# Pacing token scatters and gathers beside attention by a raw-product signal in place of a score signal

## What is computed

```python
x = x + 0.5 * _L0_ffn_ref(_layernorm(x), gate_w, expert_bias, w1, w2)
x = x + _L0_attn_ref(_layernorm(x), Wq, bq, Wk, bk, Wv, bv, Wo, bo, prior_lambda)
x = x + 0.5 * _L0_ffn_ref(_layernorm(x), gate_w, expert_bias, w1, w2)
...
# attention: 16 heads of 8 channels
scores = jnp.einsum('bhqd,bhkd->bhqk', Q, K) / math.sqrt(hd)
scores = scores + prior_lambda * _gaussian_mask(Lx)[None, None, :, :]
attn = jax.nn.softmax(scores, axis=-1)
...
# experts: 8 real ones and 4 that pass x through, the best 2 per token
topk_logits, topk_idx = jax.lax.top_k(logits, TOP_K)
```

## Time and profile before

| | us |
|---|---|
| median of 3 runs | 1354.19 |
| lowest and highest run | 1350.55, 1358.74 |
| span of the profiled execution | 1338.4 |
| TensorE, VectorE, ScalarE, GpSimd busy in it | 1003.1, 906.0, 716.5, 621.8 |

### The profile page before, as it was taken

The page is one execution under the profiler, slowest core; times in us unless marked ns, Lnnn a source line. Parts: engine busy times, 40 slices in busy tenths (PEclk is TensorE's granted clock), DMA queues, the critical chain, the costliest instruction groups (busy, mean ns, idle before and its releaser), DMA issues.

```text
span 1338.4 us, 37494 instructions
## 1 busy us (share of the span) xinstructions
PE 1003.1 (75%) x13558; PEld 656.9 (49%) x13558; DVE 906.0 (68%) x2405; ACT 716.5 (54%) x1486; POOL 621.8 (46%) x697
## 2 busy tenths in 40 slices
PE   1468587788778888888888888898888876774770
PEld 1346243475447544574444754454754465433560
DVE  4548776685566787866887758877867853654524
ACT  1157344567355755667556575555675555442650
POOL 2556256404544544354542544544445445543554
PEclk9989699998788999998999889988999987785886
DMA  8354535352135311362112731123621274130464
GB/s 247 78 125 107 152 98 173 70 131 55 58 68 131 84 52 60 82 149 60 48 58 65 141 87 53 47 61 73 137 81 53 62 162 113 48 90 19 110 145 113
DMA packets 248881, 125.30 MB, mean 94 GB/s; under 512 B 124384, under 2 KB 238925, under 8 KB 248448
## 3 DMA queue, kind: packets, MB, share of 16 engines
q1 hardware_dynamic: 232320, 94.01, 27.2%
q0 software_dynamic: 16384, 28.89, 8.9%
HBM read 36.25 MB, written 65.31 MB: 76 GB/s over the span
## 4 chain that ended last, share of the span: by engine, by line
PE 39%; DVE 27%; issue 15%; ACT 8%; another core or an unknown queue 7%; POOL 2%; DMA 1%; SPq 1%; DVEq 0%; POOLq 0%; ACTq 0%
PE banks L594 10%; DVE row_max L1329 9%; PE banks L623 4%; PE banks L569 3%; ACT probs L849 3%; DVE h_lo L1223 3%; PE banks L561 2%; PE banks L474 2%; ACT h_hi L778 2%; PE banks L431 2%; PE banks L472 2%; PE banks L487 2%; PE banks L490 2%; DVE stats L1094 2%
## 5 line engine op out<-in xcount | busy, mean ns | idle before, releaser
L849 ACT ACTIVATE probs<-banks 128x512 f32<-128x512 f32 x512 | 280.1, 595 | 313.0 <-PE banks L594 270.4
L1329 DVE TENSOR_REDUCE row_max<-banks 128x2 f32<-128x512 f32 x512 | 330.9, 685 | 100.5 <-PE banks L594 65.2
L938 POOL DMA_INDIRECT big<-yg,slots x256 | 255.2, 997 | 278.3 <-ACT y_rows L784 84.0
L924 POOL DMA_INDIRECT xg<-xs,slots x256 | 253.6, 991 | 274.7 <-PE banks L594 167.8
L1223 DVE TENSOR_TENSOR h_lo<-h_f,h_hi 128x512 bf16<-128x512 f32 x198 | 134.5, 688 | 156.7 <-ACT h_hi L778 118.5
L623 PE MATMUL banks<-probs,v_op 128*32 128x256 f32 x2048 | 202.2, 413 | 10.7 <-ACT ot_sb L842 3.0
L569 PE MATMUL banks<-q_op,k_op 32*128 32x256 bf16 x1024 | 152.2, 293 | 64.7 <-issue 46.0
L594 PE MATMUL banks<-band_parts,thirds 96*32 96x296 bf16 (+2 forms) x4096 | 189.7, 294 | 1.3 <-issue 1.3
L487 PE MATMUL banks<-w_all,h_hi 128*128 x792 | 157.6, 229 | 43.1 <-DVE h_lo L1223 21.6
L561 PE MATMUL banks<-k_op,q_in 32*128 32x256 bf16 x1024 | 154.7, 295 | 37.8 <-DVE row_max L1329 31.5
L776 ACT ACTIVATE h_f<-banks 128x512 f32<-128x512 f32 x198 | 119.8, 605 | 114.3 <-PE banks L474 71.5
(11 more groups left out here) (173 smaller groups left out, 1668.6 us busy)
## 6 DMA issues: line engine op xcount, KB each, us to landing
yg<-y_rows SPq DMA_DIRECT2D x198, 128.0 KB
k_op<-kq_kept SPq DMA_DIRECT2D x96, 64.0 KB
q_in<-kq_kept SPq DMA_DIRECT2D x96, 64.0 KB
xg<-zeros SPq DMA_DIRECT2D x2, 2944.0 KB
xg<-xs,slots POOLq DMA_INDIRECT x256
big<-yg,slots POOLq DMA_INDIRECT x256
kq_kept<-kq_hi SPq DMA_DIRECT2D x32, 128.0 KB
kq_kept<-kq_lo SPq DMA_DIRECT2D x32, 128.0 KB
```

Source lines behind the costliest of these rows:

```text
L849: act.activation(probs[:, q % 2, u % 4, :], banks[:, ST[(16 * b + u) % 3], :], ACT.Exp).then_inc(A["exp_done"], 1)
L924: pool.indirect_dma_start(xg[q], bass.IndirectOffsetOnAxis(slots[:, q % 4, c, t:t + 1], 0), xs[:, q % 2, t, :], None, bounds_check=groups[ ...
L938: pool.indirect_dma_start(y_back[:, i, c, :], None, yg[q], bass.IndirectOffsetOnAxis(slots[:, q % 4, c, t:t + 1], 0)).then_inc(gathered[i] ...
L1329: dve.tensor_reduce(row_max[:, gp, :, qt, j], banks[:, MX[v % 2], :].rearrange("p (k c) -> p k c", k=2), AX.X, ALU.max).then_inc(A["max_do ...
```

## The change

Within `spread` alone, each transfer waits for another signal. So far, if both transfers of a tile fall into one step, the first waits for the step's first score signal and the second for its second; if they fall into two steps, each waits for the second score signal of its own step. Now, if both fall into one step, they wait for the step's first and second raw-product signal; if into two, each waits for the first raw-product signal of its own step. Where no raw products are left for the step (the steps from the eleventh on after the start of turn 30), both wait for the first score signal.

```diff
-                    same = at[0] == at[1]
-                    counts = [16 * b + 2 * at[0] + (1 if same else 2), 16 * b + 2 * at[1] + 2]
-                    rows(q, t, t + 1, (A["st_done"], *counts))
+                    if 16 * b + 2 * at[1] + 12 <= 16 * NBATCH:
+                        same = at[0] == at[1]
+                        counts = [16 * b + 2 * at[0] + 11, 16 * b + 2 * at[1] + (12 if same else 11)]
+                        rows(q, t, t + 1, (A["raw_done"], *counts))
+                    else:
+                        counts = [16 * b + 2 * at[0] + 1, 16 * b + 2 * at[1] + 1]
+                        rows(q, t, t + 1, (A["st_done"], *counts))
```

## The result

The changed kernel took 1375.89 us (median of 4 runs, 1372.63 to 1384.16) against 1354.61 us for the kernel before in the same set (4 runs, 1350.55 to 1358.74). The ratio is 1.0152, with a 95% interval of 1.0107 to 1.0198: about 21 us slower. The profiled execution has a span of 1372.8 us. Executions that the record marks as slow count in the medians but not in the ratios.

A forecast was written before the change was run, and what follows sets the result against it. TensorE and VectorE were taken to bound the kernel, with GpSimd early and waiting for TensorE. Terms 0 + 0 + 0 + 0 on a 1338.4 us span, 15.8 us below the median, gave 1354 us; range 1344 to 1363.

The forecast's parts named there:

- the slower side: Measured times above 1361 us, given a chance of 0.15: most of the slower rival and as much of the forecast's tail.
- the term of traffic: Transfers beside the next sequence's operand-row loads: one random 0.92 us hold of TensorE per turn, 0 us, 5 us either way.
- The start of the transfers: Paced transfers on GpSimd: some 167 of 288 start 0.3 to 0.8 us sooner; in turn 14, within 0.9 us of first maximum.
- Ends of gathers: Gathers beside attention end up to 0.8 us sooner, three steps or more ahead of use in combine: 0 us.
- the experts' columns: Column loads behind a segment's last scatter start 0.8 us sooner, 7 us ahead of the first expert matmul: 0 us.
- What is queued behind the waits: GpSimd's next transfer and norm: at most 12 norms start sooner, meeting VectorE's column operation or not; 5.4 us either way, taken 0.
- Slower rival, operand rows: Step 0's earlier transfer delays operand rows TensorE needs in step 3: 14 us added, 1368, or 1361 with half; chance 0.14.
- Faster rival: Transfers leave the crowded end of a step: norms gain up to 5.4 us, holds 9.2 us; near 1343; chance 0.20.
- the rule weighed with it: GpSimd and VectorE lock a shared port pair; transfers belong beside maxima, not combine. By the rule alone, time stays 1354.
- What would make it wrong: The prediction's last sentence: a hold of TensorE that no row names follows the timing of the transfers.
- the smaller signs: GpSimd's busy time falls by under 20 us, chain share near 2%; VectorE's and TensorE's busy times the same to 1%.

The follow-up runs named there:

- experiment A: The change applied to step 7's transfers alone, and to all but step 7's; against the kernel before in a 1350 us set: ratios 1.0103 and 1.0004.
- the last kernel: The changed kernel with GpSimd's norm moved behind step 6's transfer, against the kernel before at 1356.31 us: 1353.11 us, ratio 0.9988.
- the probe: Not the kernel: TensorE runs 5,952 matmuls that wait for nothing while GpSimd issues spaced scatters, gathers, stores and adds; 658.32 us in a 1350 us set.
- e4_after: The changed kernel, unaltered, in a set of the 1210 us kind: 1209.13 us against 1209.17 for the kernel before, ratio 0.9996.

## Why the prediction was wrong

The forecast of 1354 us with a range to 1363 missed 1375.89. It had the slower side at 0.15. The step that failed is the term of traffic, put at 0 us with 5 us either way as one hold of TensorE at a random place in each of thirty turns. The runs show 12 turn ends at which the merge waits 10 us in sum for a late signal of TensorE, a lower clock behind them, and a loss of 14 us when step 7's transfer alone is moved. Point by point:

- *The start of the transfers.* Right. At the step of turn 14 that answers to the earlier trace rows the maxima start at 671.92 and the transfer at 672.68, 0.76 us behind; under 0.9 was predicted.
- *Ends of gathers, the experts' columns.* Right as far as seen: VectorE waits for gathers 8 times, 13.0 us in all, against 8 times and 12.9 us. GpSimd's share of the chain stays 2%.
- *What is queued behind the waits.* This is where a correct reading stopped short. The prediction saw that step 6's transfer comes 0.17 us behind the norm and "doesn't move at all". It didn't draw the next line: step 7's, behind it in the same queue, does move, from 2.13 us behind step 6's (669.08 - 666.95) to 1.35 us. One of eight steps has its transfers brought together by the change, and experiment A puts about 14 of the 21 us there.
- *Traffic, bounded by turns with and without transfers.* This is the term that was mis-sized. I read from the earlier trace rows that transfers cost a turn one hold of at most 0.92 us, and called its place random, so that thirty turns gave 5 us either way. It isn't random: whether a transfer costs depends on which of TensorE's signals is due behind it and who waits for that. Turn after turn has the same order of work, so the sign is the same in each; a sum by the square root of 30 had no ground. The turn I chose, 16, had the pattern in it, in a view that the prediction doesn't show. Around its one hold, from 694.67 to 697.57, GpSimd's timeline before has two transfers 1.28 us apart, and the raw product that ends the hold was done at 696.65 and signalled at 697.55:

```profile
695.53 0.97 POOL L924 DMA_INDIRECT xg<-xs,slots  x1 [2.60 <-PE banks L594]
696.81 0.97 POOL L924 DMA_INDIRECT xg<-xs,slots  x1 [0.30 <-issue]
```

  Measured: 0.84 to 0.92 us at the merge in each of ten turns. The eight turns behind eight of these are 1.0 us longer each, and the prediction had no term for the clock at all.
- *Slower rival, operand rows.* Right in sign, and its 14 us (15 x 0.92) are near the 21 us by luck, since the mechanism is wrong. TensorE waits for the rows of L376 once for 0.6 us and once for 0.2 us after the change, as before.
- *Faster rival, and the rule weighed with it.* The Trainium skill's page "SBUF — State Buffer" (the section on two separate sides) has GpSimd and VectorE lock one another out of a shared pair of ports. The rows agree in a small way: the column operation takes 0.20 us in the last kernel, with no norm beside it, and 0.36 us before, beside the norm's application. That is 0.16 us, and no run shows it to move the time of the kernel. The page's other rule, that GpSimd can't write its descriptors, is for VectorE's two-port operations; the combine was not shown to be one, so the transfer of 1.05 us beside it, in place of 0.98, doesn't bear that rule out. The late signals aren't this: the probe's gaps come behind transfers with no operation of two SBUF inputs beside them.
- *What would make it wrong.* The last sentence named it: a hold of TensorE that no row names and that follows the timing of the transfers. More precisely, it is a delay of its signals. Rows for it were at hand: ScalarE at 668.26, idle for 2.71 us, 0.8 us after the matmuls it waited for had ended. In that trace 141 of ScalarE's 252 starts of an exponential out of an idle time come over 0.3 us behind the score tile's last matmul; in e4_after 2 of 224. I had looked at the transfers' releasers, not at how long after its producer each waiter starts. Of the smaller signs, two failed: TensorE's busy time grew by 2.2%, where 1% was given, and GpSimd's grew by 3.5 us, where it should fall.

What stays open. Why TensorE's signals are late in some sets and not in others isn't known. It isn't the number of the chip: the chip listed under one number gave 1209 us in one set and 1356 us in another. The probe's gaps are in records, and nearly every execution on record has a span and a granted clock of its own, so it was recorded while it ran; whether the recording takes part in the delay, no run shows. That the late signals explain the whole difference of some 145 us between the kinds wasn't tested. And the step from the delayed merge to the lower clock rests on the windows of four kernels, two with the late merges and two without, and not on an experiment of its own.

## What to carry to other kernels

When a change moves an instruction in a queue, write out the next two in that queue as well: the harm came from the neighbour that moved because the first one couldn't. For each waiter near the moved work, compare its start with the end of its producer, not only the name of its releaser; an engine that starts 0.8 us after its input is ready is a cost that no busy time shows. A shift that repeats in every turn has one sign in all of them, so its bound is the count times the price, not the root of the count. A gap in the records of signals is not a late signal until somebody who waits for it is seen to start late. And a small gain measured in one kind of set says nothing for the other.

## What the runs showed of the hardware

- In the traces of three sets and of the first comparison, TensorE's signals come late behind indirect DMAs that GpSimd starts, and the engines waiting for them start late: ScalarE at 668.26 and 688.80, 1.31 and 1.34 us behind transfers at 666.95 and 687.46. Signals of ScalarE and VectorE came in time in the same stretches. TensorE's matmuls went on every 109 ns in the probe. In the traces of the four other sets this is all but absent: 2 to 10 of some 2,000 signals come 0.3 us late or more, against 404 to 578.
- In the probe of such a set, records of signals of all three engines are missing behind each of 24 indirect DMAs, all of them from 0.8 to 1.1 us after its start, though ScalarE's signals came in time: its next copies started 33 to 38 ns behind the end of the copies they waited for. Plain stores by GpSimd and its adds left no gap.
- Behind two such transfers 1.35 us apart, TensorE's signals came out in order and 0.7 to 0.8 us apart: 2.0 us from the end of the turned columns to the merge, 1.49 us behind the second transfer.
- The changed kernel took 1209.13 us in one set, at a mean granted clock of 0.934 in the profiled execution, and 1375.89 us in another, at 0.873.
- An idle time of TensorE of 1.96 us, where it had been 0.98 us, was followed by 4 us at a granted clock of 0.67, where it had been 1.00.
